# Adding the causal mask of the second attention on VectorE instead of by products on TensorE

## What is computed

```python
q = (h @ Wq).reshape(B, S, HEADS, hd)
c = h @ Wdkv
k = (c @ Wuk).reshape(B, S, HEADS, hd)
v = (c @ Wuv).reshape(B, S, HEADS, hd)
scores = jnp.einsum('bqhd,bkhd->bhqk', q, k) / jnp.sqrt(jnp.asarray(hd, h.dtype))
causal = jnp.tril(jnp.ones((S, S), bool))
scores = jnp.where(causal, scores, jnp.asarray(-1000000000.0, h.dtype))
a = jax.nn.softmax(scores, axis=-1)
out = jnp.einsum('bhqk,bkhd->bqhd', a, v).reshape(B, S, D)
```

## Time and profile before

| | us |
|---|---|
| runs | 4437.58, 4444.02, 4462.45; median 4444.02 |
| profiled execution | 4449.35, span of its instructions 4447.6 |
| mixer and first attention | from about 100 to 2190 of the span |
| second attention | from about 2286 to 3303 (32 samples) |
| routing | to about 3890 |
| experts and merge | to the end |

### The profile page before, as it was taken

The page is one execution under the profiler, slowest core; times in us unless marked ns, Lnnn a source line. Parts: engine busy times, 40 slices in busy tenths (PEclk is TensorE's granted clock), DMA queues, the critical chain, the costliest instruction groups (busy, mean ns, idle before and its releaser), DMA issues. The chain is left out here.

```text
span 4447.6 us, 68697 instructions
## 1 busy us (share of the span) xinstructions
PE 3605.0 (81%) x23984; PEld 2589.9 (58%) x23985; DVE 1925.4 (43%) x4789; ACT 1436.8 (32%) x2809; POOL 1108.8 (25%) x899
## 2 busy tenths in 40 slices
PE   2999999999999999999869999999961111199992
PEld 1666666666666666666546666666641111199992
DVE  3444544454454454445334444444442222144442
ACT  0333333333333333333224444444431110044441
POOL 2333233233223223323210100000001222244441
PEclk7999989989999998999779999999985555599996
DMA  2000000000000000000000000000022113144448
GB/s 61 6 15 14 14 7 14 14 7 14 14 7 14 14 8 13 14 14 7 8 20 24 25 24 24 26 22 28 22 74 88 54 55 123 47 74 77 76 76 252
DMA packets 143471, 165.53 MB, mean 37 GB/s; under 512 B 20163, under 2 KB 124100, under 8 KB 143414
## 3 DMA queue, kind: packets, MB, share of 16 engines
q1 hardware_dynamic: 108918, 121.13, 8.9%
q0 software_dynamic: 25968, 35.15, 4.8%
q10 hardware_dynamic: 8528, 8.52, 0.5%
HBM read 83.81 MB, written 80.93 MB: 37 GB/s over the span
## 5 line engine op out<-in xcount | busy, mean ns | idle before, releaser
L584 ACT ACTIVATE R<-psA 128x1024 f32<-128x1024 f32 x256 | 262.2, 1024 | 664.0 <-PE psA L1016 664.0
L2126 PE MATMUL psR<-identd,d_tn 128*128 128x128 f32 x130 | 31.1, 425 | 392.8 <-DVE d_tn L2053 392.8
L1031 PE MATMUL psA<-PR,V 128*64 128x258 f32 x2048 | 316.0, 434 | 0.0
L748 DVE TENSOR_TENSOR PR<-R 128x1024 f32<-128x1024 f32 x256 | 312.8, 1222 | 0.0
L1606 DVE TENSOR_REDUCE m_nm<-psC 128x4 f32<-128x516 f32 (+1 forms) x256 | 234.1, 957 | 151.9 <-PE psC L1731 151.7
L1016 PE MATMUL psA<-qT,kT 32*128 32x256 f32 x2048 | 296.1, 407 | 0.6 <-ACT R L584 0.6
L1066 PE MATMUL psA<-wout,OT 128*128 128x256 f32 x1024 | 255.0, 398 | 16.5 <-DVE OT L790 16.5
L2126 PEld LDWEIGHTS psR<-identd,d_tn 128*128 128x128 f32 x130 | 25.9, 224 | 394.6 <-DVE d_tn L2053 394.6
L978 PE MATMUL psA<-wv,xT 128*128 128x512 f32 x512 | 250.7, 613 | 0.0
L1520 ACT ACTIVATE m_PT<-psC 128x768 f32<-128x768 f32 x256 | 193.6, 808 | 152.0 <-PE psC L1755 152.0
L1016 PEld LDWEIGHTS psA<-qT,kT 32*128 32x128 f32 x2048 | 179.0, 189 | 105.0 <-issue 90.1
(11 more groups left out here) (382 smaller groups left out, 8182.1 us busy)
## 6 DMA issues: line engine op xcount, KB each, us to landing
e_x<-xg SPq DMA_DIRECT2D x143, 129.0 KB
xraw<-in_x SPq DMA_DIRECT2D x64, 256.0 KB
odd_rows<-zeros SPq DMA_DIRECT2D x66, 128.0 KB
d_x<-xs SPq DMA_DIRECT2D x13, 640.0 KB
f_even<-out_rows SPq DMA_DIRECT2D x13, 640.0 KB
f_odd<-odd_rows SPq DMA_DIRECT2D x13, 640.0 KB
out_rows<-f_even ACTq DMA_DIRECT2D x13, 640.0 KB, 5.6
hs<-h SPq DMA_DIRECT2D x32, 256.0 KB, 2.1
```

Of the source, the lines that this page charges most:

```text
L584: act.activation(R[:, p % 2], ps[:, 0:2, :].rearrange("p a (t n) -> p a t n", t=LT), ACT.Relu).then_inc(relu_done, 1)
L748: dve.tensor_tensor(PR[:, p % 2, :, :, 0:L], R[:, p % 2], R[:, p % 2], ALU.mult).then_inc(prob_done, 1)
L1031: last = pe.matmul(ps[64 * hh:64 * hh + 64, 2 + p % 2, 0:QCOLS], V[:, d, t, n * DV:(n + 1) * DV], PR[:, p % 2, hh, t, :], start=False, sto ...
```

## The change

The products of identity and mask go. The first product of the scores into each bank (t = 1) now opens the accumulation by itself, and the one of t = 0 finds its columns cleared and overwrites them. DVE then adds the mask in place in PSUM, for four heads in one instruction (128 partitions, 4 x 128 elements), once for t = 1 and once for t = 0, and only then takes the two maxima, in the same order. Each maximum waits for its own addition by a new semaphore, `masked`. PE's two waits for the powers of the group before (`exp_done`), which stood ahead of the first and the third mask product, now stand both ahead of the scores.

```diff
             def maxima(i, g):
+
                 dve.wait_ge(s_done, 4 * i + g + 1)
-                for t in range(LT):
+                mask = v.causal_q[:, 0].unsqueeze(1).to_broadcast([P, 4, P])
+                for t in (1, 0):
+                    c = P + 1 if t else SEQ + 1
+                    dve.tensor_tensor(ps[:, 0:4, c:c + P], ps[:, 0:4, c:c + P], mask, ALU.add).then_inc(masked, 1)
+                for t in (1, 0):
                     cols = slice(0, SEQ) if t else slice(SEQ, SEQ + 1 + P)
+                    dve.wait_ge(masked, 2 * (4 * i + g) + 2 - t)
                     dve.tensor_reduce(nm[:, t, :, DK], ps[:, 0:4, cols], AX.X, ALU.max,
                                       negate=True).then_inc(max_done, 1)
...
-                for h in range(4):
-                    if h % 2 == 0:
-                        need(pe, exp_done, 2 * n - 1 + h // 2)
-                    pe.matmul(ps[:, h, P + 1:3 * P + 3].rearrange("p (a n) -> p a n", a=2)[:, :, 0:P], v.ident_bf[:],
-                              v.causal_q[:], start=True, stop=False, skip_group_check=True)
+                for b in range(2):
+                    need(pe, exp_done, 2 * n - 1 + b)
                 for t in (1, 0):
...
                         last = pe.matmul(ps[:, h, cols], qT[rows, d, g, t * P:(t + 1) * P], kT[rows, d, g, 0:keys_t],
-                                         start=False, stop=True, skip_group_check=True)
+                                         start=t == 1, stop=True, skip_group_check=True)
```

More of the change, by code:

```diff
@@ L1370, in latent_attention @@
         (pad_done, preset, h2_loaded, vc_loaded, stored, ln_stats, rooted, y_done, kept, hn_done, hn_T, hT_done, lat_done,
-         cT_done, k_done, k_copied, v_done, v_copied, q_done, q_copied, kcls_done, pool_step) = sems(
+         cT_done, k_done, k_copied, v_done, v_copied, q_done, q_copied, kcls_done, pool_step, masked) = sems(
             nc, ctx, "m_pad_done", "m_preset", "m_h2_loaded", "m_vc_loaded", "m_stored", "m_ln_stats", "m_rooted",
             "m_y_done", "m_kept", "m_hn_done", "m_hn_T", "m_hT_done", "m_lat_done", "m_cT_done", "m_k_done",
-            "m_k_copied", "m_v_done", "m_v_copied", "m_q_done", "m_q_copied", "m_kcls_done", "m_pool_step")
+            "m_k_copied", "m_v_done", "m_v_copied", "m_q_done", "m_q_copied", "m_kcls_done", "m_pool_step", "m_masked")
         (s_done, max_done, nm_done, qx_done, t_done, c_done, exp_done, pc_done, pv_done, o_copied, back_done, rec_done,
```

## The result

The changed kernel took 4559.2 us (median, 4558.67 to 4560.73) against 4443.3 for the kernel before beside it (4437.58 to 4462.45): a ratio of 1.0254, 95% interval 1.0228 to 1.0280. It is slower by about 116 us, where 196 had been forecast; the time lies inside the range.

The account below looks back on a forecast made before the run. The prediction took the chain through DVE, as long as PE's cover, to bound the second attention beside PE. 104 us of chain plus 92 us of clock falls on 4449 gave 4645, forecast as 4640 us, range 4525 to 4750.

Parts of the forecast that it names:

- What bounds the kernel: Second attention: scores, maxima on DVE and turning are already as long as PE's cover, so PE is not the only bound.
- A: Time the two DVE additions put between scores and maxima in each group: 1.25 us, from 1.20 to 1.54.
- The groups: Cost per group of a sample: 0.72, 0.72, 1.20 and 0.61 us; 3.25 a sample, 104 us over 32 samples.
- The price of the low clock: Second attention: each us at the low clock level loses 0.41 us.
- The number of falls: Half of PE's 128 holes followed by a clock fall: 64 x 3.5 = 224 us at the low level, costing 92 us.
- the clock that stays up: Rival: no clock falls behind the holes, only 98 to 141 us come, 4545 to 4585, about 4548 us; chance 0.20.
- PE as the bound: Rival: DVE's chain has room at the turning of the maxima, PE's 68 us show, gain up to 56 us; chance 0.03.
- What would show it: New profile: additions 0.68 to 0.70 us, holes 1.1 to 1.7, second attention 1120 us or more, mean clock 0.83 to 0.95.

Follow-up runs that it names:

- e1: Changed kernel without the two additions and with a mask of zeros in the scores by keys, so no causal mask inside the diagonal blocks; 4395.0 us, ratio 0.9877.
- e4: Changed kernel with PE masking queries 0 to 127, DVE adding the mask for the others only, and the unmasked maximum taken first; 4486.5 us, ratio 1.0082.
- e6: Changed kernel with a third addition: the mask of queries 128 to 255 added twice and their maximum taken last; 4740.4 us, ratio 1.0648.
- e2: Changed kernel with DVE's fetch of the output moved behind the maxima and the lowering of group 2's queries; 4566.5 us, ratio 1.0262.
- e3: Changed kernel with six unread PE products in every hole, ahead of the wait for the maxima; 4536.4 us, ratio 1.0198.
- e10: Changed kernel with PE's work spread evenly, but in group 1 PE adds the mask and the latent goes back ahead of the scores; 4418.9 us, ratio 0.9943.

## Why the prediction was right, and where it was off

- *What bounds the kernel*: right. PE at 959 of 970 us looked like the bound, but the distances in rows 3 said that the chain through DVE ended no earlier. The additions came into that chain and the saved PE time went into holes. Without any addition a sample is 1.56 us shorter than before (1.5 expected), with half of them 1.20 longer, with both 2.93, and a third adds 0.59 a group (e1, e4, e6).
- *A*: 1.25 was taken, from the fetch of the output as the nearest row; 1.21 was measured; the 0.04 for the new wait did not show. The two additions last 1.30 together at 0.69 each, so the second starts 0.61 after the first. The prediction read 1.38 out of the Trainium skill, "VectorE: DVE Perf Modes", section "The DRAIN you can't avoid"; that section also says that a next operation which is not held starts earlier, and the 0.61 agree with this.
- *The groups*: 0.72, 0.72, 1.20 and 0.61 were forecast, 0.60, 0.76, 1.10 and 0.47 measured; 94 us instead of 104. The smaller A explains 0.04 of each. Group 2 as the dearest, because of the fetch, was right, and e1 shows why. For the rest e1 gives the parts: the earlier scores were worth 0.44 in groups 0 and 1 and not 0.53, and the additions showed for 1.04 and 1.07 us in groups 0 and 3 and not for 1.21. What hid the other 0.15 there is not shown.
- *The price of the low clock*: 0.41 us for each us was worked out, 0.43 measured here and 0.42 in e6.
- *The number of falls*: this is the term that was mis-sized. "I take half of the holes to be followed by a fall: 64 x 3.5 = 224 us at the low level" became 14 falls and 58 us: 20 us of time instead of 92. The share came from the first attention, whose whole low time was put down to its 86 waits for DVE. The mean length of those is 101 / 86 = 1.17 us, that of the holes here 138.7 / 128 = 1.08: alike, and yet they yield 3.5 us at the low level each there and 58 / 128 = 0.45 here. So the low time there does not belong to such waits alone, or hangs on what stands between them. The clock's record in the trace of the kernel before has 57 spells at the low level there, of 3.4 or 6.8 us: fewer than the 86 waits, and 7 of them begin with no idle time of PE over 0.8 us in the 5 us ahead. No run took the first attention apart. Within the second attention the yield was 0.45 us a hole in the changed kernel, 89 / 128 = 0.69 in e2 and 300 / 128 = 2.3 in e6: it is no number that can be carried from stage to stage. The one hole of like length in the very stage, 1.36 us without a lower mean, was the better witness and got too little weight.
- *The rivals*: the 4559 measured lie within the time named for the clock that stays up (4545 to 4585, chance 0.20), and below the forecast's own 4594 to 4732 (chance 0.67). The whole range held because it was drawn to take that rival in. But the clock did not stay up: e3, which keeps it up, is some 23 us faster. By the practical rules of "TensorE: Matmul & The Clock Gate" in the Trainium skill, section "Why this matters for your kernels", no hole here would be long enough; the stretches above show a fall behind a hole of 1.15 us, so here the measurement decides. PE as the bound fell with e1 to e4. With other cover it comes true in part: in e10 an estimated 0.65 to 0.83 of the 1.59 us that PE saves in a sample show.
- *What would show it*: the additions as described (694 ns, starts 0.6 apart), the holes of 1.08 to 1.57 us as named (1.1 to 1.7), DVE named by all 128 waits, the stage 114 us longer where 103 were the least, and the other stages unchanged. Only the mean clock, 0.98, lay outside the 0.83 to 0.95 named.

## What to carry to other kernels

An engine that is busy 99% of a stage need not be its bound: look at the moment when it takes up another engine's result, and if that follows the result by only 0.05 to 0.2 us in every group, work moved to that other engine costs nearly its full length (1.04 to 1.20 of 1.21 us here). The same move pays once the busy engine has enough other work between giving and taking: here the change alone lost 2.5%, with PE's work spread evenly it cost nothing, and with the poorest group left out the kernel gained 0.6%, part of it by the order itself (one of its moves, made alone and in one more group, gave 0.2%). What new holes of TensorE cost in clock is best given as a range and then measured: 0.6 us more of hole brought five times the falls (14 to 76).

## What was not expected of the hardware

The falls of the clock followed no simple count of holes. In steady samples, holes of 0.48 to 0.86 us (read at the loading of weights) brought none (e4); of 1.08 to 1.57 us, one in every third sample, always behind the hole of group 1, though the same hole in the two samples between brought none; with one of the four holes shortened by half a us, two in every three samples (e2); with all of them at 1.7 to 2.2 us, 76 in the stage (e6). So it is neither length nor number alone. That three samples took 105.80 us in the changed kernel and 105.81 in e2, whose samples are 0.50 us shorter at the full clock, says that where the holes lie in time counts. In all three kernels the pattern of falls repeats every third sample, after 105.8 us in the changed kernel and in e2 and after 122.9 us, with seven falls, in e6; each fall lengthens its sample and so moves all later holes, which can bring the falls into such a rhythm. That this is how it comes about is not shown by these runs. Six unread products a hole stopped the falls at no cost that shows: PE has 66 us more of work in 20 us less of stretch (1037.10 busy in 1100 us against 971.54 in 1120), and the sample is not longer (34.70 against 34.78).
